# Masked attention in blocks of 32 live keys with the queries on the partitions, inside a fused transformer kernel

## What is computed

```
q, k, v = (proj(Wq), proj(Wk), proj(Wv))          # heads of 16
scores = einsum('bhsd,bhtd->bhst', q, k) * scale
scores = where(mask, -inf, scores)                # mask[s, t], the same for both batches
attn = softmax(scores, axis=-1)
out = einsum('bhst,bhtd->bhsd', attn, v)
out = out.transpose(...).reshape(B, S, E) @ Wo.T  # then a norm, a modulation, the experts
```

## Time and profile before

| what | value |
|---|---|
| median of 3 runs | 998.95 us |
| span of the profiled execution (its only time shown) | 994.2 us |
| PE busy | 891.8 us, 90% |
| PE weight loads | 761.0 us, 77% |
| DVE busy | 733.3 us, 74% |
| ACT busy | 407.0 us, 41% |
| POOL busy | 408.0 us, 41% |
| mean granted PE clock | 0.962 |

### The profile page before, as it was taken

How to read it: one execution, slowest core, us unless ns; L and a number is a source line. 1 busy time by engine, 2 the same in 40 slices (tenths; PEclk the granted TensorE clock), 3 DMA queues, 4 the chain that set the end, 5 groups by cost and what they waited for, 6 DMA issues and landing times. The chain is left out here.

```text
span 994.2 us, 18094 instructions
## 1 busy us (share of the span) xinstructions
PE 891.8 (90%) x5701; PEld 761.0 (77%) x5710; DVE 733.3 (74%) x1440; ACT 407.0 (41%) x776; POOL 408.0 (41%) x481
## 2 busy tenths in 40 slices
PE   7799999999937886798996899888899999999998
PEld 4799999999936676587785655456688888888887
DVE  5888888888836798768687856457676777767676
ACT  5566566666516534332246355668311111111110
POOL 3377777777742003266417522400233333332222
PEclk9899999999978996899998999999999999999999
DMA  8346113135125000420008900001001010101002
GB/s 293 123 128 213 42 42 127 42 128 180 43 77 181 0 1 1 119 85 1 1 1 147 181 3 2 1 1 33 1 17 32 16 32 16 32 16 32 16 0 84
DMA packets 50300, 61.82 MB, mean 62 GB/s; under 512 B 8014, under 2 KB 37768, under 8 KB 50248
## 3 DMA queue, kind: packets, MB, share of 16 engines
q1 hardware_dynamic: 43464, 43.85, 14.1%
q0 software_dynamic: 6336, 17.31, 7.2%
q10 hardware_dynamic: 448, 0.01, 0.0%
HBM read 47.26 MB, written 7.60 MB: 55 GB/s over the span
## 5 line engine op out<-in xcount | busy, mean ns | idle before, releaser
L2207 POOL TENSOR_TENSOR kTh<-at_acc,kTh 128x512 fp32r<-128x512 f32 x68 | 88.2, 1297 | 257.0 <-DVE kTh L2380 257.0
L2133 ACT ACTIVATE at_acc<-psum 128x512 f32<-128x512 f32 x68 | 40.6, 599 | 240.1 <-PE psum L1930 240.1
L2462 DVE SCALAR_TENSOR_TENSOR y<-psum,at_pT,y 128x256 f32<-128x256 f32 x272 | 112.2, 475 | 0.0
L1972 PE MATMUL psum<-at_wkh,kTh 128*128 128x256 f32 x544 | 107.7, 282 | 3.0 <-DVE y L2462 3.0
L1930 PE MATMUL psum<-act_hi,at_wkh 128*128 128x512 f32 x272 | 108.4, 399 | 0.3 <-ACT at_acc L2133 0.3
L1930 PE MATMUL psum<-act_hi,at_wkl 128*128 128x512 f32 x272 | 107.7, 396 | 0.0
L1930 PE MATMUL psum<-act_lo,at_wkh 128*128 128x512 f32 x272 | 107.5, 395 | 0.0
L468 ACT ACTIVATE e_u<-psum,e_bias 128x256 f32<-128x256 f32 x152 | 63.8, 471 | 95.3 <-PE psum L373 95.1
L2377 DVE TENSOR_TENSOR at_acc<-psum,at_acc 128x512 f32<-128x512 f32 x68 | 47.0, 692 | 74.4 <-PE psum L1930 61.0
L1972 PEld LDWEIGHTS psum<-at_wkh,kTh 128*128 128x128 f32 x544 | 88.8, 190 | 7.0 <-DVE y L2462 3.0
L1972 PE MATMUL psum<-at_wkl,kTh 128*128 128x256 f32 x272 | 76.5, 281 | 0.0
(11 more groups left out here) (507 smaller groups left out, 2832.8 us busy)
## 6 DMA issues: line engine op xcount, KB each, us to landing
e_raw<-in_W SPq DMA_DIRECT2D x16, 512.0 KB, 5.1
e_raw<-in_W SPq DMA_DIRECT2D x8, 1024.0 KB, 5.8
v_tok<-in_xT SPq DMA_DIRECT2D x4, 512.0 KB, 9.4
y<-in_x SPq DMA_DIRECT2D x4, 512.0 KB, 10.1
y<-y_rows SPq DMA_DIRECT2D x4, 512.0 KB, 7.3
v_tok<-y_rows SPq DMA_DIRECT2D x4, 512.0 KB, 8.1
v_tok<-in_x SPq DMA_DIRECT2D x4, 512.0 KB, 7.8
e_raw<-in_w_gate SPq DMA_DIRECT2D x16, 128.0 KB, 2.1
```

The costliest lines, as they stand in the source:

```text
L1972: last = pe.matmul(ps[4 + j][:, 0:D], hh[a][:, s % HS, j * P:(j + 1) * P], e2_w[par][b][:, OD:OD + D], start=n == 0, stop=n == 2)
L2133: act.activation(sl_sb[:, s % 2, :], ps[s % 2][:, :], ACT.Silu).then_inc(esil, 1)
L2207: pool.tensor_tensor(hh[1][:, s % HS, :], h32[:, s % 2, :], hh[0][:, s % HS, :], ALU.subtract).then_inc(hsp, 1)
L2462: dve.scalar_tensor_tensor(out=y[:, i, :], in0=ps[4 + j][:, 0:D], scalar=comb[:, i, bass.ds(2 * t + out_s // G, 1)], in1=y[:, i, :], op0=A ...
```

## The change

All of it is in the attention part and in what feeds it.

- Live keys are found in blocks of 32 (`KB`), 32 blocks instead of 8 tiles. The count in `stage_feed_forward` writes 32 sums per row; the sort takes four `max` and three `match_replace`.
- The stacked query tiles and their DMAs are gone. Queries lie whole in `q_hi`, `q_lo` (128 rows: 8 heads of 16). Keys are made block-diagonal (`ks`): for each head 32 columns that are zero outside that head's 16 rows (`own8`). One matmul of 256 columns serves 8 heads; three passes and two halves make 6, and one more adds the mask.
- `scores` are made once per tile of 128 queries (16 tiles `i`). DVE takes the maximum, subtracts it (`shift`) into `z`, ACT exponentiates `z` in place, PE turns it (`turn_weights`), ACT copies it to `pT` (`weights_out`), and `values` multiplies it by block-diagonal values `vb` (68 columns for 4 heads, with a column for the sum) in plain fp32. DVE adds into `acc`.
- `invert` is DVE's, `normalise` POOL's. `acc` is set to zero by POOL and, in its sum column, to `pen` by DVE, before the loop.
- The mask of a block is read from the copy that the feed-forward stage has loaded; SP loads nothing in the loop. High and low parts of the block's tokens are copied from `act_hi`, `act_lo` instead of being turned again.

```diff
-                def scores(j, a):
-                    ...
-                def turned_scores(j, t, k):
-                    ...
+                    def project_keys(j):
+                        pe.wait_ge(xhi, j + 1)
+                        pe.wait_ge(xlo, j + 1)
+                        for c in range(KC):
+                            for i, (k, (w_, x_)) in enumerate((k, p) for k in range(KC) for p in PASSES):
+                                last = pe.matmul(ps[7][:, c * B * KB:(c + 1) * B * KB], wk[w_][:, k, c * P:(c + 1) * P],
+                                                 xt[x_][:, k * B:(k + 1) * B, 0, :], start=i == 0, stop=i == 3 * KC - 1)
+                        last.then_inc(kps, 1)
+                    def scores(j, i):
+                        ...
+                        pe.wait_ge(zed, j * NI + i + 1)
+                        pe.matmul(bank, identb[:, :], mb[:, u, :].unsqueeze(1).to_broadcast([P, NH, KB]), start=True, stop=False)
+                        ...
+                        for a, h in ((0, 0), (1, 0), (0, 1)):
+                            for c in range(KC):
+                                last = pe.matmul(bank[:, c * HC * KB:(c + 1) * HC * KB], qs[a][:, c, i * P:(i + 1) * P],
+                                                 ks[h][:, c * B + b, :, :].rearrange("p h t -> p (h t)"),
+                                                 start=False, stop=h == 1 and c == KC - 1)
+                        last.then_inc(sps, 1)
+                    def turn_weights(j, i):
+                        pe.wait_ge(pex, j * NI + i + 1)
+                        pe.wait_ge(ptc, j * NI + i + 1)
+                        for n in range(4):
+                            last = pe.transpose(ps[3 + i % 2][:, n * P:(n + 1) * P], z[:, i % 3, n * P:(n + 1) * P], ident[:, :])
+                        last.then_inc(tps, 1)
+                    def values(j, i):
+                        ...
+                        pe.wait_ge(ptc, j * NI + i + 3)
+                        pe.wait_ge(added, j * NI + i + 1)
+                        for n in range(4):
+                            last = pe.matmul(ps[5 + i % 2][:, n * HB * (HD + 1):(n + 1) * HB * (HD + 1)], pT[:, i % 2, n * P:(n + 1) * P],
+                                             vb[:, b, n, :, :].rearrange("p h e -> p (h e)"), start=True, stop=True)
+                        last.then_inc(pvps, 1)
+                    with pe.Fori(0, n_blocks) as j:
+                        pe.wait_ge(added, j * NI + 2)
+                        project_keys(j)
+                        project_values(j, 0)
+                        for i in range(2):
+                            scores(j, i)
+                        for i in range(NI):
+                            if i + 2 < NI:
+                                scores(j, i + 2)
+                            turn_weights(j, i)
+                            if i:
+                                values(j, i - 1)
+                            ...
+                        values(j, NI - 1)
 ACT
+                        for i in range(NI):
+                            exponentials(j, i)
+                            if i:
+                                weights_out(j, i - 1)
+                            factor(j, i)
 POOL
-                            for pl in range(HC // 2):
-                                pool.dma_start(stacked(c * (HC // 2) + pl)[copy * 32:(copy + 1) * 32, b * S:(b + 1) * S],
-                                               src[pl * 32:(pl + 1) * 32, c, b * S:(b + 1) * S]).then_inc(q_in[unit], 16)
+                    pool.memset(acc[:, :, :, :], 0.0).then_inc(zeroed, 1)
+                        spread_keys(j)
+                        for i in range(NI):
+                            move(j, i)
+                            scale(j, i)
+                            if i >= 4:
+                                normalise(j, i - 4)
+                        for i in range(NI - 4, NI):
+                            normalise(j, i)
 DVE
+                        block_lo(j)
+                        keys_lo(j)
+                        spread_keys(j)
+                        values_out(j, 0)
+                        for i in range(NI):
+                            maximum(j, i)
+                            if i >= 4:
+                                invert(j, i - 4)
+                            new_maximum(j, i)
+                            if i >= 3:
+                                add(j, i - 3)
+                            shift(j, i)
```

More of the change, by code:

```diff
@@ new lines, in stage_attention @@
+                own8, own4 = sbl("at_own8", [P, HC]), sbl("at_own4", [P, HB])
+                vb = sbl("at_vb", [P, B, 4, HB, HD + 1])
+                z, pT = sbl("at_z", [P, 3, GT]), sbl("at_pT", [P, 2, GT])
+                acc = sbl("at_acc", [P, NI, NH, HD + 1])
+                mb, identb = sbl("at_mb", [P, QT, KB], BF16), sbl("at_identb", [P, P], BF16)
+                one, idle = sbl("at_one", [P, P]), sbl("at_idle", [P, 1])
+                mn, mx, df, rc = (sbl(f"at_{x}", [P, NI, NH]) for x in ("mn", "mx", "df", "rc"))
@@ L1632, in stage_attention @@
                 mod, junk = take(B, 2 * D), take(2, 2, D)
-                z, sc, rep = (take(NT, E2) for _ in range(3))
+                lg, sc, rep = (take(NT, E2) for _ in range(3))
                 comb, top = take(NT, E2 + 1), take(NT, 8)
@@ L2005, in _ @@
-                    for u in range(QE, 2 * NU):
+                    act.activation(identb[:, :], ident[:, :], ACT.Copy).then_inc(id16, 1)
+                    for u in range(QE, NQP):
                         query_high(act, q_hi, u, qps, qhi)
-                        if u == 2 * NU - 4:
-                            act.wait_ge(counted, 1)
-                            copy_tile(0)
-                        if u == 2 * NU - 2:
-                            tile_hi(ps[4], 0)
-                    flat = acc[:, :, :, :, :].rearrange("p b u h e -> p (b u h e)")
@@ L2185, in _ @@
-                    n = live_tiles(pool)
-                    with pool.Fori(0, n) as j:
-                        pool.wait_ge(added, j * NBT + 1)
-                        move(j, 0)
-                        for t in range(NBT):
-                            scale(j, t)
-                            if t % NV == 1 and t // NV + 1 < NU:
-                                move(j, t // NV + 1)
-                    pool.wait_ge(m_in, 16 * (n + 1))
-                    pool.tensor_tensor(done[:, :], one[:, 0:1], one[:, 0:1], ALU.add)
+                    pool.memset(own8[:, :], 1.0).then_inc(cset, 1)
@@ new lines, in _ @@
+                    ch.link(dve.reciprocal(pen[:, :], cnt[:, :]))
+                    ch.link(dve.tensor_scalar(pen[:, :], pen[:, :], 0.0, None, ALU.mult))
+                    dve.wait_ge(zeroed, 3)
+                    dve.tensor_copy(acc[:, :, :, HD].rearrange("p (b u) h -> p b u h", b=B),
+                                    pen[:, :].unsqueeze(1).unsqueeze(3).to_broadcast([P, B, QT, NH])).then_inc(zeroed, 1)
+                    for u in range(QE, NQP):
+                        query_lo(u)
@@ L2480, in adaln_block @@
         rows = sb("rows", [P, 4, D])
-        free = rows[:, 3, 9 * NT:9 * NT + QT * QT].rearrange("p (q j) -> p q j", j=QT)
         bkv, gb = rows[:, 0:2, :].rearrange("p n d -> p (n d)"), rows[:, 2:4, :]
```

652 lines of the change are left out of this document (202 added, 450 removed).

## The result

The changed kernel takes **922.99 us** (median of 4 runs, 922.27 to 923.82), the kernel before, run beside it, 999.12 us (4 runs, 998.25 to 1002.16): 0.9238 of the time, 95% interval 0.9217 to 0.9259. The forecast was 927.3, the range 913 to 950. The profiled execution took 922.40 us with a span of 920.7, so 1.7 us lie around the span.

What follows compares the result with a forecast made beforehand. PE was taken to bound the loop: first scores at 543.9 + 37.9 loop + 4 clock = 585.8 instead of 657.4, 71.6 us less, so 998.95 - 71.6 = 927.3 us; range 913 to 950.

Steps and rivals of the forecast that it cites:

- Bound and trips: Attention loop: PE bounds its middle, and only one trip runs, one block of 32 live keys.
- Part 2: A tile of the loop: PE is the longest engine at 2.2 us, 16 times; the loop takes 37.9 us with filling.
- The small turns: Value products in a tile: lower end of their cost, loads about 0.065 us apart, 0.52 us in all.
- Part 1: Ahead of the loop: sort, loop entry, key products and spreads put the first scores at 543.9, 0.4 us earlier than before.
- Part 3: Clock at the start: 8 us of the loop at half speed add 4 us; ends 0 and 8.
- filling and end: Loop's ends: 3.5 us filling, 1.1 for the last copy and tail, minus 1.9 for two tiles without scores behind them.
- Part 4: Behind the loop: output products 0 and 1 start 5.5 and 10.1 us after the last values; gain taken as 0.
- All later work keeps its length, since PE bounds it: Everything later, behind the loop: its length stays the same, so no time is gained or lost.
- The ring of GpSimd and ScalarE: Rival in the loop: their hand-over sets the pace, a tile takes 2.8 us, 9.6 us more, 937; chance 0.20.
- Half clock throughout: Rival in the loop: all PE work doubles, a tile takes 4.4 us, total 958; chance 0.12.
- The tiles overlap as ordered: Against the rival that loop tiles do not overlap, 6.5 to 9.2 us each, about 1030 us; chance 0.02.
- the loop runs once: Against the rival of more trips through the loop, each costing 40 us and more; chance 0.01.

Runs made afterwards that it cites:

- v1: The changed kernel with exponentials and values rounded to fp32r before their product, so a value product is one instruction, not two; 921.62 us.
- w1: The changed kernel with 22 unread products more in TensorE's waits: behind the last query product, ahead of the keys, behind the value projection; 922.87 us.
- q1: The changed kernel with GpSimd idle while VectorE sorts, ScalarE zeroing the accumulators and VectorE's last low query parts made before `pen`; 921.38 us.
- c1: The kernel of q1 with GpSimd's key spreads waiting for VectorE's, and the first tile's scores waiting at first only for the high keys; 918.43 us.
- b1: The kernel before the change with only the split weights of the last experts moved, into the tile that held queries; 998.25 us.
- c2: The kernel of c1 with 17 unread products more, all ahead of the key products; 919.03 us.
- t4: The changed kernel with its loop run four times instead of once, going through 128 keys; 1066.77 us (one run).
- c3: The kernel of c2 with exponentials and values rounded to fp32r ahead of their product; 912.99 us.
- d1: The kernel of c3 with seven unread products more in the waits at the end of the loop; 911.63 us.

## Why the prediction was right, step by step

**Bound and trips** (right). TensorE bounds the middle before and after; one trip, 16 reductions.

**Part 2, the tile** (right, to the hundredth). Mask and scores 0.92 us against 0.94, turns 0.43 against 0.44, values 0.85 against 0.85; 2.20 as forecast. The choice of the turn as the nearest row for the value products was the one that counted. Eight instructions take 0.85 us, and four of the same columns in v1 take 0.45. Each costs 0.11 with 68 moving columns, as much as a turn with 128 (four in 0.43) or a key product of w1 with 64 (0.111); what they share is weights of 128 rows by 128 columns, so the weights set it and not what moves. By the rule of the Trainium skill (TensorE: Matmul & The Clock Gate, LDWEIGHTS), 107 ns a load, it is 0.85 too; the trace agrees here. The small turns, whose weights have 16 rows, did not carry over, and their 0.065 was read too low: four loads in 0.32 us are 0.08 each, so the lower end for the values was 0.64 and not 0.52.

**Part 1, ahead of the loop** (wrong by 6 us: the scores start 22.8 us after the start of the part, and 16.8 were forecast). Four terms were too small: the sort, held up by GpSimd, 2.6; the entry of the loop, 1.92 in place of 0.6, 1.3 (that the register reads take it is argued, no run takes them out); the key products, all at half clock, 0.7; the spreads, 2.7 in place of 1.5, again the two engines in each other's way, 1.2. q1 and c1 show the first and the last. "If the register load is dearer or the clock low, 3 us later" named two of them, and both came. That VectorE and GpSimd hold each other up was not on the list.

**Part 3, the clock** (mechanism right, size too large). The clock was 0.51 for the 10 us into the loop and back by about 554. It lay mostly over the key products and the first two tiles, so the loop itself took 38.97 us instead of 37.9 + 4. This gave 2.9 us back. The 1.1 us over 37.9 are not the clock alone: by w1 the half clock costs 1.3 at the first two tiles, and the sum had left out the second value projection, six products in the fourth tile from 562.72 to 563.52, which sets two reductions 2.90 us apart (561.76 and 564.66) and not 2.20. So the other terms, filling and end, must have been some 0.9 too large.

**Part 4, behind the loop** (0 forecast with 2 either way; 3.3 gained). Product 0 starts 4.1 us after the last values (594.19 less 590.09) where 5.5 was forecast, product 1 8.9 (598.97) where 10.1 was; at product 1 that is 1.7 us less than the 10.6 of the kernel before. That GpSimd's split would release product 0 was right, and it came sooner since GpSimd's divisions took 0.6 us each and not 0.75:

```profile
588.82 2.94 POOL L1988 TENSOR_TENSOR v_tok<-at_acc,at_rc 128x256 f32<-128x256 f32 x5
591.71 1.09 POOL L2007 TENSOR_TENSOR at_wqh<-cd_raw,at_one 128x512 fp32r<-128x512 f32 x1
592.88 1.26 POOL L2010 TENSOR_TENSOR at_wql<-cd_raw,at_wqh 128x512 fp32r<-128x512 f32 x1
```

```profile
594.19 0.39 PE L1748 MATMUL psum<-at_wqh,act_hi 128*128 128x256 f32 x1 [0.20 <-POOL at_wql L2010]
```

The other 1.6 us come behind product 1. The clock has 0.95 of them: in the kernel before it was down here, which I had not looked up, and in the changed one it stays at 1.00, so that the second half of product 1 started 3.28 us after the first (671.29 less 668.01) and now starts 2.33 after it (601.30 less 598.97). The last 0.6 show as a shorter wait for ScalarE's copy ahead of the second half of product 2 (1.38 us at 678.13, 0.67 at 607.52); why it is shorter is not shown. The kernel before, around its product 1:

```profile
667.00:672.00 5.00, 4.09 (x25) 4.00 (x25) 4.69 (x12) 2.71 (x11) 0.00 (x0) 0.73 0.01 3
```

**"All later work keeps its length, since PE bounds it"** (wrong by 2.9 us). The products of 512 columns in the last experts follow each other 2% faster. Unexplained, as told above.

**The sum.** By stages the span should have fallen by 71.6 and fell by 73.5: 1.3 (start) + 5.9 (scores) - 2.9 (clock) - 3.3 (behind the loop) - 2.9 (experts) = -1.9. Another 2.4 us come from the step from span to median. I took 4.75 us around the span from the median of the runs before, but in every run that shows both it is 1.7 to 2.0 (922.40 less 920.7; 1000.11 less 998.1 for b1). The profiled execution of the kernel before was simply one of its quicker ones, and a difference of single executions carries some 3 us of chance. The errors were of both signs, so that the forecast came within 4.3 us of the median is luck in part: Part 1 alone was 5.9 off. The range was put together loosely: values at 1.0 and 8 us of half clock give 927.3 + 2.4 + 4 = 934, 936 with the tail, and not 938.

**The rivals.** The ring of GpSimd and ScalarE does not set the pace: GpSimd waits and in the loop nobody waits for it, and in v1 the same ring turns in 1.76 us. Half clock throughout did not come; neither did the swinging of a loop through psum banks that the Trainium skill (TensorE: Matmul & The Clock Gate, "A second HAM failure mode") describes, with 0.99 in the steady loop. At the loop's two ends, where TensorE waits, the clock did come down in some kernels: 0.51 behind the wait of 4.0 us at the entry, and 0.82 in c2 but 1.00 in c1 behind the same waits at the exit. The tiles overlap as ordered, and the loop runs once; t4 shows that each further trip costs 48 us, so by an estimate from it the change would lose with three live blocks that lie in one tile of 128 (923 + 96 = 1019).

## What to carry to other kernels

Cost each instruction of the steady loop from the row nearest to it in the shape of its weights, rows and columns; here the sum then held. The errors sat at the entry and the exit of the loop, where waits, the entry itself and the clock add up term by term. When small steps of VectorE take a microsecond, compare their ends with the ends of GpSimd's instructions, and move GpSimd's work out of a chain that others wait for. After every edit that shortens a stage, read the granted clock of the stage behind it: v1, c2 and c3 each gave 1.5 to 3.7 us back there.

## What was not expected of the hardware

- VectorE's instruction on 8 numbers of a row took 0.17 us alone and 1.30 beside GpSimd's subtraction of 512 (q1); two spreads took 0.75 alone and 1.58 beside GpSimd's.
- The clock falls or stays with the same waits: behind the last values TensorE waited 1.09 us and 0.20 us in both c1 and c2, and the stretch had 1.00 and 0.82. Seven products of 0.23 us that nobody reads, put into the waits, took it from 0.51 to 1.00 (d1 against c3).
- The first instruction of a loop on VectorE came 1.9 us after the last one ahead of it, the same in the changed kernel and all built from it (1.90 to 1.92), with nothing to wait for that the profile shows.
- Products of 512 columns at full clock came every 0.234 us in one program and every 0.229 in another, in the expert steps between 800 and 850 us.
